# Value minus error on GpSimd from SBUF instead of on VectorE from PSUM, in a delta-rule attention kernel

## The reference

```python
x = _layernorm(x)
rk = x.reshape(B, T, H, d);  rk = rk / max(norm(rk), 1e-12)
wk = rk shifted by one token
v = x @ Wv.T;  gate = sigmoid(x @ Wg.T);  beta = sigmoid(x @ Wb.T)
def step(S, inp):
    pred = einsum('bhk,bhkd->bhd', wk_t, S)
    err = (v_t - pred) * b_t[..., None]
    S = S + wk_t[..., None] * err[..., None, :]
    o = einsum('bhk,bhkd->bhd', rk_t, S) * g_t[..., None]
out = scan(step) @ Wo.T          # then layernorm, residual, feed-forward part, layernorm, residual
```

## Time and profile before

| | |
|---|---|
| three runs | 2714.48, 2715.66, 2721.57 us |
| the profiled execution, its own time | 2721.43 us |
| its span | 2719.3 us, granted TensorE clock 0.917 in the mean |
| TensorE busy | 79% |
| VectorE busy | 88% |
| ScalarE busy | 52% |
| GpSimd busy | 47% |

### The profile page before, as it was taken

How to read it: one execution, slowest core, us unless ns; L and a number is a source line. 1 busy time by engine, 2 the same in 40 slices (tenths; PEclk the granted TensorE clock), 3 DMA queues, 4 the chain that set the end, 5 groups by cost and what they waited for, 6 DMA issues and landing times. The chain is left out here.

```text
span 2719.3 us, 147410 instructions
## 1 busy us (share of the span) xinstructions
PE 2149.1 (79%) x60965; PEld 1381.0 (51%) x60965; DVE 2398.8 (88%) x7114; ACT 1403.1 (52%) x2988; POOL 1271.2 (47%) x2457
## 2 busy tenths in 40 slices
PE   2688878888878888888888888888888874777776
PEld 1355555555555555555555555555555542444343
DVE  4689999999989898999999999998999956787775
ACT  3445555555555455555555555554555334555554
POOL 1324444444444344444444444443444323777777
PEclk6789999999999898999999999998999877888888
DMA  2112222222222222222222222222222214656554
GB/s 78 47 48 64 73 68 69 71 67 67 66 66 66 66 66 66 67 66 74 63 72 66 74 64 69 67 70 63 68 78 57 63 42 137 158 156 157 155 144 93
DMA packets 132134, 215.58 MB, mean 79 GB/s; under 512 B 31352, under 2 KB 31360, under 8 KB 131488
## 3 DMA queue, kind: packets, MB, share of 16 engines
q1 hardware_dynamic: 131488, 206.20, 26.8%
HBM read 104.40 MB, written 67.11 MB: 63 GB/s over the span
## 5 line engine op out<-in xcount | busy, mean ns | idle before, releaser
L517 POOL TENSOR_TENSOR o_g<-pred,gate 128x512 f32<-128x512 f32 x128 | 134.1, 1048 | 1100.3 <-DVE pred L802 1100.3
L699 DVE TENSOR_TENSOR ps_elim<-ps_elim,sys 128x30 f32<-128x30 f32 (+14 forms) x1920 | 546.1, 329 | 7.8 <-issue 7.0
L875 PE MATMUL ps_v<-wv,xt 128*128 128x512 f16 x1536 | 436.3, 417 | 133.7 <-DMA kbd<-kt 123.6
L707 DVE TENSOR_TENSOR sys<-sys,ps_elim 128x30 f32<-128x30 f32 (+14 forms) x1920 | 538.5, 320 | 1.0
L875 PE MATMUL ps_y<-wo,ot 128*128 128x512 f16 x1536 | 389.4, 389 | 25.4 <-issue 19.5
L1246 PE MATMUL ps_f<-wq,f_xq 128*128 128x512 f16 x1024 | 280.8, 425 | 102.4 <-ACT f_yn L1122 98.4
L890 PE MATMUL ps_chain<-state,key_t 32*32 32x32 f32 x16384 | 206.6, 197 | 147.4 <-issue 146.6
L875 PEld LDWEIGHTS ps_v<-wv,xt 128*128 128x128 f16 x1536 | 137.9, 103 | 346.7 <-issue 198.7
L920 PEld LDWEIGHTS ps_chain<-rhs,t_t 32*32 32x32 f32 x16384 | 249.6, 145 | 75.4 <-issue 72.3
L890 PEld LDWEIGHTS ps_chain<-state,key_t 32*32 32x32 f32 x16384 | 177.3, 108 | 214.3 <-issue 211.3
L920 PE MATMUL ps_chain<-rhs,t_t 32*32 32x32 f32 x16384 | 266.9, 218 | 18.6 <-issue 11.2
(11 more groups left out here) (152 smaller groups left out, 4693.3 us busy)
## 6 DMA issues: line engine op xcount, KB each, us to landing
x_in<-in_L_attn_x SPq DMA_DIRECT2D x128, 256.0 KB
kbd<-kt SPq DMA_DIRECT2D x512, 64.0 KB
x_res<-in_L_attn_x SPq DMA_DIRECT2D x128, 256.0 KB
x_scratch<-x SPq DMA_DIRECT2D x128, 256.0 KB, 6.3
f_x<-x_scratch SPq DMA_DIRECT2D x32, 1024.0 KB, 7.6
out<-f_res SPq DMA_DIRECT2D x128, 256.0 KB, 4.0
gate<-gates SPq DMA_DIRECT2D x128, 7.9 KB
gate<-gates SPq DMA_DIRECT2D x128, 0.2 KB
```

Source lines behind the costliest of these rows:

```text
L517: pool.tensor_tensor(heads(o_g[:, l % 2, :]), heads(pred[:, :]), spread(gate[:, l, :]), ALU.mult).then_inc(s["o_done"], 1)
L699: dve.tensor_tensor(tmp, factors(r, c, first, end)[:, c - first:C - 1 - first, c - first:c - first + 1].to_broadcast(shape), sys[:, r, c:c ...
L707: dve.tensor_tensor(dst, dst, tmp, ALU.add).then_inc(elim_done[r], 1)
L875: last = pe.matmul(out, lhs[:, a, kb, :], weights[:, w, kb, :], start=(i == 0), stop=(i == 3 * KB - 1))
```

## The change

GpSimd takes pred = value - err from the SBUF copy err that ScalarE has made, right ahead of o_g, so VectorE no longer reads ps_chain a second time. GpSimd waits for err_done instead of pred_done from VectorE. The copy to err gets a wait for o_done of n - 1, because err has two buffers that GpSimd now reads. TensorE's chain_ready no longer waits for pred_done, because after ScalarE's copy nobody reads the bank ps_chain.

```diff
@@ gpsimd, step
                 n, l, live = on(base, j, 0)
                 if live:
+                    wait(pool, s["err_done"], n + 1)
+                    wait(pool, s["o_done"], n)
+                    pool.tensor_tensor(pred[:, :], val[:, l, :], err[:, l % 2, :], ALU.subtract).then_inc(s["pred_done"], 1)
                     wait(pool, s["pred_done"], n + 1)
                     wait(pool, s["ot_psum"], n - 1)
                     wait(pool, gate_done[l], eights(base, j, 0) * 16 + 16)
@@ scalar, step
                     wait(act, s["err_psum"], n + 1)
+                    wait(act, s["o_done"], n - 1)
                     wait(act, s["s_psum"], n - 1)
@@ vector, step
-                n, l, live = on(base, j, 0)
-                if live:
-                    wait(dve, s["err_done"], n + 1)
-                    wait(dve, s["o_done"], n)
-                    dve.tensor_tensor(pred[:, :], val[:, l, :], ps_chain[:, :], ALU.subtract).then_inc(s["pred_done"], 1)
-
@@ tensor, chain_ready
                 if live:
-                    wait(pe, s["pred_done"], n)
                     wait(pe, s["state_done"], n + 1)
                     wait(pe, s["keyt_done"], n + 1)
```

## The result

The changed kernel is slower by a little: 2725.41 us against 2714.59 us (medians of 20 runs each), ratio 1.0036 with a 95% interval of 1.0021 to 1.0052. Measured again beside the first experiments, it was 1.0057 (1.0031 to 1.0082). I had forecast 2712 and no change. One execution of the kernel before, beside the last three experiments, took 9758 us and is left out of their ratios.

What follows compares the result with a forecast made beforehand. VectorE's and TensorE's loops were taken as nearly equal. Collisions of 60 us against 64 saved in 108 steps, about half counting, plus 1 us for TensorE's wait, gave -4 us: 2712 us, no measurable change (own range 2707 to 2724, whole 2692 to 2738).

Steps and rivals of the forecast that it cites:

- What bounds the kernel: Attention loop: VectorE's and TensorE's loops are nearly equal; TensorE's mostly sets the pace, VectorE's in stretches ending in m_t waits.
- rival 1: Collisions at z_ends are cheap or fall where VectorE would idle: up to 18 us faster, 2698 us; chance 0.30.
- The removed instruction: VectorE's subtraction on line 802, once a step: 0.59 us each, 75.5 us for 128.
- ScalarE's wait: Before ScalarE's copy to err, for o_done of n-1: costs nothing, at most 13 us in all.
- The collisions with z_ends: VectorE lines 787 and 789 against GpSimd's pred and o_g: 60 us in 108 steps, 0.56 a step.
- the whole-duration bound: Upper bound at z_ends if each blocked operation waits by whole durations: 90 us in 108 steps, 0.83 a step.
- The cap of 0.76 us an operation: Most a collision costs a VectorE operation, from f_z's 1.29 us median less its 0.53 minimum.
- What else could collide: VectorE's other work near z_ends has one input in PSUM, so no collision cost was taken there.
- The sum: VectorE's load changes by -5 us in 128 steps, about half counting; with 1 us for TensorE's wait, -4 us.
- The steadying effect: At z_ends: a VectorE that falls behind collides less, one that runs ahead collides more; no size given.
- The signs: z_ends mean 0.95 to 1.0 us, VectorE's idle before rhs within 15 us; wrong if other VectorE lines stretch.
- rival 2: Each z_ends (lines 787, 789) waits for a whole GpSimd operation: VectorE +31 us, time 2731 to 2746; chance 0.25.

Runs made afterwards that it cites:

- the two kernels without z_ends: Both z_ends operations and ScalarE's two waits for them removed, constants instead: on the changed kernel 0.9885, on the kernel before 0.9912.
- the one with o_g held: Changed kernel with GpSimd's o_g waiting until the second z_ends is done, pred left free: ratio 0.989 of the kernel before.
- the one with both held: Changed kernel with GpSimd's pred and o_g waiting for the second z_ends, and o_g also for g_den: ratio 0.989 of the kernel before.
- pred twice: Kernel before with VectorE's pred subtraction done twice, the second waiting for the first: ratio 1.0291.
- pred on GpSimd as well: Kernel before with the subtraction added on GpSimd, VectorE's pred kept and ScalarE's new wait included: ratio 1.0026.
- z_ends earlier: Changed kernel with z_ends moved ahead of the second third of the elimination: ratio 1.0099; the same move on the kernel before: 1.0002.

## Why the prediction was wrong, by its own steps

*What bounds the kernel* was right: two loops of nearly one length. The floor under VectorE's gain, rival 1's -18 us, was of the right kind and somewhat too high: the two kernels without z_ends, the one with o_g held and the one with both held lie 21 to 32 us under the kernel before by their medians. Where the few us beyond TensorE's waits for m_t come from stays open. TensorE's "issue" pauses before the chain product did not grow: 145.2 us in the kernel with only o_g held, 146.6 before.

*The removed instruction* was right, 75.5 us, once nothing collides. *Pred's duration on GpSimd* was right: 1.26 taken, 1.27 in the median. *ScalarE's wait* cost nothing that could be measured, as taken.

*The collisions with z_ends* failed in size: this is the first of the two steps that broke the sum. The time from the first z_ends to ot is 1.20 us in the kernel before, whatever err does; in the changed one, over 112 steps (rhs at 302.19 the first, at 2146.28 the last), sorted as in the prediction, with what it took and what was measured beyond the 1.20 (us):

| err ends after rhs | steps | taken | measured |
|---|---|---|---|
| up to 5.9 us | 31 | 0 | 0.02 |
| 5.9 to 6.95 | 39 | 0.4 | 0.56 |
| 6.95 to 8.25 | 26 | 1.1 | 1.27 |
| 8.25 to 8.9 | 11 | 0.76 | 1.50 |
| later | 5 | 0 | 1.08 |

In the mean 0.69 us a step, where I took 0.56 and the whole-duration bound was 0.83. (My count was off as well: between the two rhs of the earlier trace rows lie 112 steps and not 108, in the five classes 24, 40, 37, 6 and 5. It moves my 0.56 only to 0.55.) The whole durations (0.52, 1.70 and 1.26) on the changed kernel's own counts would have given 0.70, though class by class they miss in both directions. The cap of 0.76 us an operation, from f_z beside f_res, was the wrong neighbour: a blocked z_ends took up to 1.77 us, 1.08 more than free. The nearest row was f_veps, which waited out all of f_xq, and it was the one to go by. The Trainium skill's rule that I named beside the upper bound ("SBUF — State Buffer", "Who interferes with whom": the second to issue is blocked until the first has ended) agrees: in the step at 1099.24 the first z_ends ended 0.55 us behind pred and the second 0.54 us behind o_g, and so did all 114 that were held.

*What else could collide* failed in kind, and is the second step ("The rest of VectorE's work near there (elimination, m_t, x1, ot, xt) has one input in PSUM"). The prediction looked only at operations with two inputs in SBUF and only between err and 2.47 us later. G_den has one. In the changed kernel 23 of its 128 were longer than 0.3 us, 22 of them across key, which GpSimd starts earlier now because o_g is earlier (13.2 us after rhs in the median before, 12.6 now), a move that the prediction had priced at nothing. It adds 16.6 us to VectorE. The same page says, in the same section, that tensor_scalar can enter 2-port modes, if its operands meet the conditions, and can then contend with GpSimd; the runs agree (137 to 702 ns when o_g crosses it), and it would have pointed at g_den.

*The sum*: with 0.69 a step and g_den's 0.13, VectorE's load changes by (0.69 + 0.13 - 0.59) x 128 = +29 us, where I had -5; its busy time shows +23.2. Of the 34 us between the two sums each of the two steps has half. That about half of a change in load arrives in the time was right for a rise of this size (10.8 of 23 to 29 us), but it is no constant. Downwards, 38.5 us less busy time gave 25 us, 75 gave 32, and 154 us of load 21; upwards, 82 of 90 us arrived with pred twice and 10 of 27 with pred on GpSimd as well, and with z_ends earlier the time rose by 1% at the same busy time.

*The steadying effect*, that a VectorE which falls behind collides less, is too weak: the steps with an err early enough to collide with nothing went from 24 to 31 of 112 only.

*The signs* that the prediction named were a mixed guide. The mean of z_ends, 1.0 us, lies at the top of the 0.95 to 1.0 that went with its own sum, and VectorE's idle time before rhs stayed within 15 us; the sign that spoke was "if other VectorE lines stretch", which g_den did. Outcome and mechanism are those of rival 2, which had 0.25, at two thirds of its price; but of the net rise of 29 us in VectorE's load, 17 are g_den, which it did not have. Whether TensorE's missing wait for pred_done gives its 1 us was not isolated.

## What to carry to other kernels

Before an operation is moved to GpSimd, list what VectorE does in the whole stretch in which GpSimd's work will now run, the work behind the moved operation included, and mark every VectorE operation that has two SBUF inputs or is an SBUF-to-SBUF tensor_scalar, the two kinds that were held here: each that overlapped cost nearly the rest of GpSimd's operation, however short it was itself. Then place the two by a wait, so that they don't overlap; here a wait on the engine with time to spare turned +0.4% into -1.1%. And look for the bend: where two loops are nearly equal, less load gains only down to the other loop's floor (20 to 30 us here, however much is taken away), while more load can cost nearly all of itself.

## What the runs showed of the hardware

A VectorE operation of 32 elements a partition, 0.14 us alone, takes 0.70 us when a GpSimd operation of 512 elements is under way, and a z_ends of 0.68 us takes up to 1.77: the wait is for GpSimd's operation and not in proportion to VectorE's. GpSimd in turn was held when VectorE was first: its ln_sc addition of one element went from 0.19 to 0.63 us in the median of the changed kernel, and the 73 that were held all ended 0.05 us behind a z_ends. Operations with an input in PSUM were hardly touched: the 3840 products and sums of the elimination took 1084.6 us before and 1086.1 after. Nor were two others from SBUF to SBUF with one input: the gates' reciprocal took 0.353 us in the median, in the 31 steps of the changed kernel in which it started inside a large GpSimd operation as in the others, and the key transposes took 0.70 us when they started inside o_g, in 119 steps of the kernel before.
